# Attention with a conditioned norm, fp32 in two pieces: scores formed twice instead of probabilities turned, and three head pairs projected ahead

## The reference

```python
# b 8, n 512, dim 1024, 16 heads of 64, all float32
scale, shift = jnp.split(emb @ W_emb + b_emb, 2, axis=-1)
xn = _rms_norm(x, g_norm) * (1.0 + scale) + shift
qkv = (xn @ W_qkv).reshape(b, n, 3, h, d)
q = _rms_norm(q, g_q); k = _rms_norm(k, g_k)
logits = jnp.einsum('bhqd,bhkd->bhqk', q, k) * d ** (-0.5)
attn = jax.nn.softmax(logits, axis=-1)
o = jnp.einsum('bhqk,bhkd->bhqd', attn, v)      # heads side by side: (b, n, dim)
return x + o + o @ W_out
```

## Time and profile before

| | |
|---|---|
| median of 3 runs | 2279.28 us (2278.8 to 2279.79) |
| the profiled execution | 2278.89 us, span 2276.0 us |
| granted TensorE clock, mean | 0.999 |
| busy: PE, PEld | 2256.2 us, 2110.3 us |
| busy: DVE, ACT, POOL | 1597.9, 1345.7, 651.7 us |
| DMA, mean | 152 GB/s |

### The profile page before, as it was taken

How to read it: one execution, slowest core, us unless ns; L and a number is a source line. 1 busy time by engine, 2 the same in 40 slices (tenths; PEclk the granted TensorE clock), 3 DMA queues, 4 the chain that set the end, 5 groups by cost and what they waited for, 6 DMA issues and landing times.

```text
span 2276.0 us, 36733 instructions
## 1 busy us (share of the span) xinstructions
PE 2256.2 (99%) x13392; PEld 2110.3 (93%) x13392; DVE 1597.9 (70%) x3284; ACT 1345.7 (59%) x3101; POOL 651.7 (29%) x880
## 2 busy tenths in 40 slices
PE   8999999999999999999999999999999999999999
PEld 4999989999999999999999999999999999999999
DVE  4898784787827778287872878738786487854875
ACT  4687772667616676176762667526674366743663
POOL 3444431324213241122312234122331223302220
PEclk9999999999999999999999999999999999999999
DMA  9544346422364332733236332362323723246331
GB/s 359 224 167 177 112 154 228 178 99 110 118 220 184 107 115 88 256 148 112 111 114 256 112 112 112 122 253 107 112 112 130 291 92 118 82 151 246 111 121 65
DMA packets 71269, 346.35 MB, mean 152 GB/s; under 512 B 7601, under 2 KB 43441, under 8 KB 47537
## 3 DMA queue, kind: packets, MB, share of 16 engines
q1 hardware_dynamic: 71088, 344.01, 41.2%
HBM read 293.65 MB, written 50.33 MB: 151 GB/s over the span
## 4 chain that ended last, share of the span: by engine, by line
PE 86%; DVE 8%; ACT 2%; issue 1%; POOL 0%; DMA 0%; ACTq 0%; DVEq 0%
PE proj_bank L502 18%; PE proj_bank L500 18%; PE proj_bank L501 18%; PE flip_bank L598 9%; PE pv_bank L609 5%; PE pv_bank L610 5%; PE score_bank L590 4%; PE score_bank L591 4%; PE flip_bank L553 2%; DVE probs L865 2%; DVE neg_max L859 2%; DVE pt_lo L869 2%; PE flip_bank L563 1%; ACT k_hi L700 1%; PE proj_bank L525 1%
## 5 line engine op out<-in xcount | busy, mean ns | idle before, releaser
L500 PE MATMUL proj_bank<-w_split,xn_hi 128*128 128x384 f32 x2048 | 700.0, 342 | 1.4 <-DVE res L907 0.8
L502 PE MATMUL proj_bank<-w_split,xn_lo 128*128 128x384 f32 x2048 | 688.5, 336 | 0.0
L501 PE MATMUL proj_bank<-w_split,xn_hi 128*128 128x384 f32 x2048 | 687.4, 336 | 0.0
L718 ACT ACTIVATE probs<-score_bank,neg_max 128x512 f32<-128x512 f32 x512 | 352.6, 691 | 213.5 <-DVE neg_max L859 211.2
L500 PEld LDWEIGHTS proj_bank<-w_split,xn_hi 128*128 128x128 f32 x2048 | 385.2, 188 | 18.1 <-DVE xn_lo L854 1.0
L501 PEld LDWEIGHTS proj_bank<-w_split,xn_hi 128*128 128x128 f32 x2048 | 385.5, 188 | 15.2
L724 ACT CAST pt_hi<-flip_bank 128x512 fp32r<-128x512 f32 x512 | 288.8, 591 | 182.0 <-PE flip_bank L598 91.1
L869 DVE TENSOR_TENSOR pt_lo<-flip_bank,pt_hi 128x512 fp32r<-128x512 f32 x512 | 339.9, 685 | 78.1 <-ACT pt_hi L724 75.9
L502 PEld LDWEIGHTS proj_bank<-w_split,xn_lo 128*128 128x128 f32 x2048 | 384.8, 188 | 0.0
L859 DVE TENSOR_REDUCE neg_max<-score_bank 128x1 f32<-128x512 f32 x512 | 341.3, 684 | 17.0 <-PE score_bank L591 13.0
L865 DVE TENSOR_SCALAR probs<-probs,row_inv 128x512 f32<-128x512 f32 x512 | 275.7, 539 | 18.1
(11 more groups left out here) (86 smaller groups left out, 3205.1 us busy)
## 6 DMA issues: line engine op xcount, KB each, us to landing
w_split<-w_store SPq DMA_DIRECT2D x140, 1536.0 KB, 7.0
w_store<-w_split SPq DMA_DIRECT2D x20, 1536.0 KB, 10.1
x_tile<-in_x SPq DMA_DIRECT2D x32, 512.0 KB, 11.0
w_raw<-in_w_qkv SPq DMA_DIRECT2D x16, 768.0 KB, 8.4
w_split<-w_store SPq DMA_DIRECT2D x12, 1024.0 KB, 5.1
w_raw<-in_x SPq DMA_DIRECT2D x56, 192.0 KB, 6.7
out<-w_raw SPq DMA_DIRECT2D x56, 192.0 KB, 1.9
emb_stage<-in_w_emb SPq DMA_DIRECT2D x5, 1024.0 KB, 10.6
```

The lines of the kernel that those rows point to most:

```text
L500: nc.tensor.matmul(dst, a_hi, w_hi, start=(kt == 0), stop=False)
L501: nc.tensor.matmul(dst, a_hi, w_lo, start=False, stop=False)
L502: mm = nc.tensor.matmul(dst, a_lo, w_hi, start=False, stop=(kt == KT - 1))
L718: nc.scalar.activation(probs[h][:, i, :], score_bank[n % 2][:, :], ACT.Exp, bias=neg_max[:, n:n + 1], accum_out=row_sum[:, n:n + 1]).then_ ...
```

## The change

A piece of 128 keys by 512 queries now comes out of a second product of q and k with the sides exchanged. The high piece of k, as the stationary operand, is multiplied with both pieces of q, and in a second matmul its low piece with a copy of q's high piece. The row maximum is taken, as before, from scores with queries on the rows, now formed by one matmul instead of two; step H turns the four columns of `neg_max` (one transpose with 4 columns of data), and DVE spreads them over four spare rows of `q_max` (each row holds the maximum of its own 128 queries, zeros elsewhere), where four rows of ones in `k_lo` add them to the turned scores. So F ends in an exponential on ACT straight from `flip_bank`, without a row sum; step E is an ACT copy to `pt_hi`, and DVE takes `pt_lo` from SBUF. Nothing is divided before the product with v. The sums over keys are made from the unsplit exponentials: step U, three adds of 128x512 on POOL per head and an ACT copy of a half; N, a DVE add of 64x512 per head; J, a split on ACT and DVE; G, a product with a matrix of ones by heads (two matmuls), a reciprocal of 128x512 from PSUM and a multiplication of `o_pair` with it, on DVE. Z is the DVE copy of `q_split` to `q_max`.

`LATE` is 3: pair 2 of the next batch (10) is also projected, and its scores taken, ahead of the output product. The first batch keeps two residual buffers instead of three, and in the last batch `y_half[0]` holds one of the residual tiles. All five tables are written anew.

```diff
-LATE = 2
+LATE = 3
...
-        2C0 2C1 2C2 2C3 2C4 2C5 2C6 2C7 2C8 2C9 2C10 2C11 2C12 2C13 2C14 2C15 3C0 3C1 3C2 3C3 2T0 2T1 3C4 3C5 3C6 3C7
...
-        first_res = [sb(f"res{i}", [P, QKV]) for i in range(3)]
+        first_res = [sb(f"res{i}", [P, QKV]) for i in range(2)]
...
                     elif kind == "S":
-                        pe.wait_ge(exp_done, it * 8 + (n - 2 + 1 + CREDIT))
+                        wait_past(pe, max_done, it * 8 + (n - 1))
...
-                        nc.tensor.matmul(score_bank[n % 2][:, :], q_t, k_hi[h][:, :], start=True, stop=False)
-                        nc.tensor.matmul(score_bank[n % 2][:, :], q_t, k_lo[h][:, :], start=False,
-                                         stop=True).then_inc(score_full, 1)
+                        nc.tensor.matmul(score_bank[n % 2][:, :], q_split[:, h, i * P:(i + 1) * P], k_hi[h][:, :],
+                                         start=True, stop=True).then_inc(score_full, 1)
+                    elif kind == "H":
+                        flip_wait(pe, u)
+                        pe.wait_ge(max_done, it * 8 + 4 * n + 4)
+                        nc.tensor.transpose(flip_bank[flip][0:TT, 0:P], neg_max[:, 4 * n:4 * n + 4],
+                                            ident[:, :]).then_inc(flip_full, 1)
                     elif kind == "F":
-                        wait_past(pe, flip_free, releases(order, u))
+                        flip_wait(pe, u)
                         if i == 0:
-                            pe.wait_ge(probs_ready, it * 8 + (4 * h + 4))
-                        for qt in range(TT):
-                            mm = nc.tensor.transpose(flip_bank[flip][:, qt * P:(qt + 1) * P],
-                                                     probs[h][:, qt, i * P:(i + 1) * P], ident[:, :])
-                        mm.then_inc(flip_full, 1)
+                            freed(pe, "H", h, it)
+                            freed(pe, "T", 1, it)
+                        nc.tensor.matmul(flip_bank[flip][:, :], k_hi[h][:, i * P:(i + 1) * P], q_split[:, h, :],
+                                         start=True, stop=False)
+                        nc.tensor.matmul(flip_bank[flip][:, :], k_lo[h][:, i * P:(i + 1) * P], q_max[:, h, :],
+                                         start=False, stop=True).then_inc(flip_full, 1)
...
+                    elif kind == "G":
+                        flip_wait(pe, u)
+                        if is_first(it):
+                            pe.wait_ge(ones_ready, 2)
+                        pe.wait_ge(sum_lo_done, it + 1)
+                        nc.tensor.matmul(flip_bank[flip][:, :], head_ones[:, :], sum_hi, start=True, stop=False)
+                        nc.tensor.matmul(flip_bank[flip][:, :], head_ones[:, :], sum_lo, start=False,
+                                         stop=True).then_inc(flip_full, 1)
...
                     elif kind == "F":
                         act.wait_ge(flip_full, u + 1)
...
+                        nc.scalar.activation(probs[h][:, i, :], flip_bank[flip][:, :],
+                                             ACT.Exp).then_inc(flip_freed["ScalarE"], 1)
+                    elif kind == "E":
                         act.wait_ge(pv_used, it * 8 + (n - 1 + CREDIT))
-                        nc.scalar.copy(pt_hi[n % 2][:, :], flip_bank[flip][:, :]).then_inc(flip_hi, 1)
...
+                        nc.scalar.copy(pt_hi[n % 2][:, :], probs[h][:, i, :]).then_inc(p_hi_done, 1)
...
+                    elif kind == "Z":
+                        freed(dve, "T", 0, it)
+                        nc.vector.tensor_copy(q_max[:, :, :], f32(q_split[:, :, :])).then_inc(q_copied, 1)
...
+                    elif kind == "F":
+                        dve.wait_ge(p_hi_done, it * 8 + (n + 1))
+                        nc.vector.tensor_tensor(pt_lo[n % 2][:, :], probs[h][:, i, :], f32(pt_hi[n % 2][:, :]),
+                                                ALU.subtract).then_inc(p_lo_done, 1)
                     elif kind == "N":
-                        dve.wait_ge(exp_done, it * 8 + (n + 1 + CREDIT))
-                        nc.vector.reciprocal(row_inv[:, n:n + 1], row_sum[:, n:n + 1]).then_inc(inv_done, 1)
-                        dve.wait_ge(inv_done, it * 8 + (n + 1))
-                        nc.vector.tensor_scalar(probs[h][:, i, :], probs[h][:, i, :], row_inv[:, n:n + 1], None,
-                                                ALU.mult).then_inc(probs_ready, 1)
...
+                    elif kind == "G":
+                        dve.wait_ge(flip_full, u + 1)
+                        dve.wait_ge(sum_lo_done, it + 1)
+                        dve.wait_ge(o_sum_done, it * 2 + (2 + CREDIT))
+                        nc.vector.reciprocal(sum_inv, flip_bank[flip][:, :]).then_inc(inv_done, 1)
+                        dve.wait_ge(inv_done, it + 1)
+                        nc.vector.tensor_tensor(o_pair[:, :], o_pair[:, :], sum_inv,
+                                                ALU.mult).then_inc(flip_freed["VectorE"], 1)
...
+            def add_keys(it, n):
+
+                head, part = n // 3, n % 3
+                e = probs[head]
+                if part < 2:
+                    pool.wait_ge(p_lo_done, it * 8 + (4 * head + 2 * part + 2))
+                    src, dst = 2 * part, 2 * part + 1
+                else:
+                    pool.wait_ge(keys_added, it * 6 + n)
+                    src, dst = 1, 3
+                op = nc.gpsimd.tensor_tensor(e[:, dst, :], e[:, src, :], e[:, dst, :], ALU.add)
+                op.then_inc(keys_added, 1)
```

More of the change, by code:

```diff
@@ L226, in flip_buf, with order_of, flip_table @@
-def flip_buf(order, kind, n, p):
-    places = HEAD_FLIPS if order is HEAD else TAIL_FLIPS if order is TAIL else BODY_FLIPS
-    before = 0 if order is HEAD else HEAD_FLIPS[1]
-    assert BODY_FLIPS[1] % 2 == 0
-    return (before + places[0][(kind, n, p)][0]) % 2
-FIRST_X = {HEAD_FLIPS[0][("X", r, 0)][0] for r in range(TT)}
-def releases(order, u):
-    return u if order is HEAD and u - 2 in FIRST_X else u - 1
+def order_of(b):
+    return HEAD if b == 0 else TAIL if b == B - 1 else BODY
+def flip_table():
+    table, releases, counts = {}, [], {"ScalarE": 0, "VectorE": 0}
+    for b in range(B):
+        for step in order_of(b)["TensorE"]:
+            p, d, kind, n = read_step(step)
+            if kind in "TFXHG":
+                table[(kind, n, b + d if kind == "X" else b * PAIRS + p)] = len(releases)
+                for owner in ("VectorE", "ScalarE") if kind == "X" else ("ScalarE",) if kind == "F" else ("VectorE",):
+                    counts[owner] += 1
+                    releases.append((owner, counts[owner]))
+    return table, releases
@@ L337, in cond_attention @@
         v_split = [sb(f"v_split{h}", [P, TT, P], F32R) for h in range(2)]
-        probs = [sb(f"probs{h}", [P, TT, T]) for h in range(2)]
+        probs = [sb("probs0", [P, TT, T])]
+        with nc.sbuf_tensor("sum_split", [P, TT, T], F32R) as sum_split:
+            pass
+        probs.append(sb("probs1", [P, TT, T]))
         pt_hi = [sb(f"pt_hi{i}", [P, T], F32R) for i in range(2)]
@@ L557, in cycle @@
                         for half in range(2):
-                            wait_past(pe, flip_free, releases(order, u + half))
+                            flip_wait(pe, u + half)
                             if half == 0:
@@ L667, in round_x, with modulated @@
                                y_half[half][:, :].rearrange("p (k t) -> p k t", k=4)).then_inc(xn_hi_done, 1)
+            def modulated(u, half):
+                owner, count = RELEASES[u + half]
+                act.wait_ge(flip_freed[owner], count)
             def xn_high(n, u, flip, r):
@@ L682, in cycle @@
                     if kind in "TFX":
-                        u = flip_at(order, b, kind, n, d if kind == "X" else p)[0]
-                        flip = flip_buf(order, kind, n, d if kind == "X" else p)
+                        u = flip_of(kind, n, b + d if kind == "X" else it)
+                        flip = u % 2
                     if kind == "V":
@@ L814, in save_mod @@
                 nc.vector.tensor_copy(by_batch[:, KT:2 * KT, :], mod_t[:, KT:2 * KT, :]).then_inc(mod_step, 1)
+                dve.wait_ge(mod_step, MOD_SAVED)
+                nc.vector.memset(f32(head_ones[:, :]), 0.0).then_inc(ones_ready, 1)
+                dve.wait_ge(ones_ready, 1)
+                for head in range(2):
+                    op = nc.vector.memset(f32(head_ones[rows(head), rows(head)]), 1.0)
+                op.then_inc(ones_ready, 1)
             def cycle(order, m, c):
@@ L911, in _ @@
             for head in range(2):
-                nc.vector.memset(f32(k_lo[head][rows(1 - head), :]), 0.0)
+                op = nc.vector.memset(f32(k_lo[head][rows(1 - head), :]), 0.0)
+            op.then_inc(k_lo_zero, 1)
+            dve.wait_ge(k_lo_zero, 1)
+            for head in range(2):
+                nc.vector.memset(f32(k_lo[head][(1 - head) * DH:(1 - head) * DH + TT, :]), 1.0)
```

436 lines of the change are left out of this document (230 added, 206 removed).

## The result

The changed kernel takes 2558.35 us (2550.86 to 2560.67, four runs), the kernel before beside it 2279.04: a ratio of 1.1221, 95% interval 1.1197 to 1.1245. It is 279 us slower. I had forecast 2261 and a range up to 2390: the sign was wrong, and the time lies outside the range.

The account below looks back on a forecast made before the run. PE's instruction stream was taken as the bound. From 2278.9 us, 61 less stream, 38 more for POOL waits and 5 for residual buffers gave 2260.9, so 2261 as median; range 2222 to 2390.

Parts of the forecast that it names:

- The step that failed first: DVE's reciprocal of 128x512 from PSUM: priced at 0.69 us, like other 512-column forms, within bounds 0.69 and 7.3.
- The forecast for that estimate: Reciprocal at the page's repeat count, 4.3 us: 2.6 us per pair reach PE, 2430 us in all.
- Rival B: Wide reciprocal on DVE is slow, 3.2 us; about 1.6 us per pair reach PE, 2363 us; chance 0.30.
- POOL's adds: Six POOL adds per pair block DVE's SBUF forms: 170 us on DVE, of which 38 us reach PE.
- Rival C: POOL waits take more than the gain, over 0.95 us per pair on PE: 2290 to 2330; chance 0.10.
- rival A: The plan swallows the POOL waits as before, so none reach PE: 2223 us; chance 0.12.
- The shorter stream: PE's instruction stream: 5.34 us per pair gone, 4.38 new, net 0.96; 61 us shorter over 64 pairs.
- rival D: PE's stream is not shortened, the same time turns up as equal waits: 2275 to 2284; chance 0.06.
- DVE's fuller stretch: DVE's work per batch falls into a narrower attention stretch: 81% busy, where it was 75%.
- with everything else unchanged ... even: DVE's load per pair: 4.9 us plus the reciprocal against 5.6, even if the reciprocal takes about 0.7.
- ACT: ACT's work per pair, exponentials, copies and splits: 12.3 us for 11.9, on an engine at 59%; cost nothing.
- The two residual buffers: First batch, loads wait for the store two tiles back: 5 us once, bounds 0 and 10.

Follow-up runs that it names:

- the three spare reciprocals: Kernel before, plus three reciprocals of 128x160 in a row per pair on VectorE, whose result nobody waits for: 2505.1 us.
- eight spread: Kernel before, plus eight unused reciprocals of 128x46 per pair on VectorE, one behind each scaling: 2366.8 us.

## Why the prediction was wrong, step by step

**The step that failed first:** "I take 0.69, the nearest rows in shape, and keep the upper end as a rival." The reciprocal takes 3.35 us. The bounds, 0.69 and 7.3, were right, and so was the reading that could have decided: 158 ns for one element against a fixed part of 144 is 14 ns an element at the most, and 6.3 was true. I let the nearest shape decide, where the only row of the same operation spoke for the other side. The Trainium skill, "VectorE: DVE Perf Modes", section "First, the fixed hardware budget", gives an iterative divide with a repeat count of 8; by that the trace agrees in kind, several cycles for each element. In size the measurement decides: the estimate from the page was 4.3 us, and by an estimate at the page's 0.96 GHz 6.3 ns are 6 cycles, not 8. The forecast for that estimate, 2430, was still 128 us too low, so the reciprocal was not the only error.

**Rival B** had the mechanism and nearly the duration (3.2 us), but its price of 1.6 us per pair, 102 us, was too low: it was 168 beside the adds and 188 without, 2.6 to 2.9 per pair. I counted one gap behind each G. What I left out shows in the rows around 1090: the flip bank is held for the reciprocal's length too, and after a gap of two us the clock falls. 49 us of the loss after is slowed matmuls, 28 with the copy, so 21 of the 168 us are the clock.

**POOL's adds.** "0.22 us per operation ... 170 us on DVE" was too much: DVE's busy time rose by 107 to 111 us. "I take 0.6 us per pair, 38 us, a quarter" was too little: 66 to 85 us, 1.0 to 1.3 per pair, of which some 30 are POOL's own queue, which the sum didn't have. POOL's busy time (1261 for 1160) was near. The rule of the Trainium skill, "SBUF — State Buffer", section "Who interferes with whom", held in the form it has there, two SBUF inputs on DVE: the low pieces reach 1.78 us. Z has one input, of 1024 columns, and rises even more, from 0.70 to 1.11; the forecast had no such price for it, though the same section counts a cast among the operations that can contend with GpSimd when they run in a two-port mode. Rival C, taken for itself (over 0.95 us per pair), came true as well, and rival A, which swallowed the adds, did not.

**The shorter stream** held: 63 us for 61, the new matmuls start 0.23 us apart, and rival D is out. H was priced at 0.109 us for each transpose and costs some 0.03: the stream is shorter by some 10 us more, which the waits took as well.

**DVE's fuller stretch.** I worked out 81% for 75% and gave it no price. The run with a copy for the reciprocal and adds of one column says 88 us for all that is left, residual buffers included; 35 of them go with a lighter DVE. This alone is more than the gain from the stream: with a division as quick as a copy and adds of one column the change still loses 26 us. This is the second failed step: "with everything else unchanged ... even" compared loads, where places in the order count. Which places they are stays open for 20 to 35 us.

**ACT** at nothing: cutting its copies to a quarter took 140 us off its busy time and gave 13 us. The change had added 29 us (1374.4 for the 1345.7 of the earlier trace rows), so what was missed is probably well below 13.

**The two residual buffers**, 5 us forecast: PE waits 4.4 us, once, behind these two on DVE (start us, us, idle before), against the earlier trace rows:

```profile
454.78 0.42 DVE L970 TENSOR_TENSOR res<-proj_bank,res 128x256 f32<-128x256 f32 x1 [9.05 <-DMA res<-in_x]
458.07 0.42 DVE L970 TENSOR_TENSOR res<-proj_bank,res 128x256 f32<-128x256 f32 x1 [2.86 <-DMA res<-in_x]
```

**The sum as it is:** -61 of stream, +88 of order and residual buffers, +85 of adds, +168 of reciprocal: 2279 + 280 = 2559.

## What to carry to other kernels

An operation that the trace shows at one width only has no price at another: bound it per element from its own row, and let the sign of the forecast follow the bound, or measure it first. A long step on an in-order engine was paid at its full length here, both where it held a bank and where nobody waited for its result, though the engine was idle for 24 to 30% of the time; the same work in pieces cost 40% of that. Before dividing a broadcast tile, count the different values in it, and count the small matmuls that the detour needs.

## What the runs showed of the hardware

- A reciprocal on DVE: 158 ns for 1 column, 204 for 8, 433 for 46, 1153 for 160, 3352 for 512. From 46 columns on that is 144 ns and 6.3 ns an element.
- Losses of PE by a long wait are followed by a second one: 2.21 us idle, then 3.4 us with starts 0.32 us apart for 0.173 and 0.43 for 0.23. In the records of the span 130 us after are at the lower clock, 164 with the three spare reciprocals, 3 before and 3 with eight spread.
- A matmul with 2 moving columns and 128 stationary ones starts 0.11 us after the last, as a transpose of 128 columns does. Behind a transpose of 4 stationary columns the next matmul starts after 0.03 us.
- A DVE cast with one SBUF input of 1024 columns suffered more from POOL's adds (0.71 to 1.11 us; with the copy for the reciprocal 0.70 to 1.20) than a subtraction with two inputs of 512 (0.72 to 0.84).
